# Three tiles of 99 tokens in place of three overlapping tiles of 128 in the variance of a normalisation

## The reference

```python
def _layernorm(x, axis=-1, eps=1e-05):
    m = jnp.mean(x, axis=axis, keepdims=True)
    v = jnp.var(x, axis=axis, keepdims=True)
    return (x - m) / jnp.sqrt(v + eps)
...
h = tokens(x)                            # normalise patches, project, normalise, + embedding
h = concatenate([cls_tok, h], axis=1)    # 16 x 37 tokens of 256 features
h = h + causal_attention(_layernorm(h))  # 16 heads, rotary embedding
h = h + experts(_layernorm(h))           # router, 16 experts that choose 74 tokens each, a shared one
h = h + encoder(_layernorm(h))           # below
h = h + fp4_ffn(_layernorm(h))           # weights and values rounded to fp4 in blocks of 16
...
def encoder(x):
    x = _ln(x, norm_in_g, norm_in_b) + pos_emb
    for l in range(6):
        q, k, v = x @ Wqkv[l].T + bqkv[l]
        o = softmax(mask(q @ k.T / 4)) @ v
        x = _ln(x + o @ Wo[l].T + bo[l], ln1_g[l], ln1_b[l])
        ff = gelu(x @ W1[l].T + b1[l]) @ W2[l].T + b2[l]
        x = _ln(x + ff, ln2_g[l], ln2_b[l])
    return x
```

## Time and profile before

| | |
|---|---|
| three runs | 821.06, 821.38 and 822.22 us |
| median of the runs | 821.38 us |
| span of the profiled execution | 819.1 us |
| PE busy | 801.5 us, 98% of the span |
| PEld busy | 751.4 us, 92% |
| DVE, ACT, POOL busy | 633.9, 460.6 and 251.6 us |
| clock granted to PE | full in all 40 slices of the page |
| DMA | 88.36 MB, 108 GB/s |

### The profile page before, as it was taken

How to read it: one execution, slowest core, us unless ns; L and a number is a source line. 1 busy time by engine, 2 the same in 40 slices (tenths; PEclk the granted TensorE clock), 3 DMA queues, 4 the chain that set the end, 5 groups by cost and what they waited for, 6 DMA issues and landing times.

```text
span 819.1 us, 16629 instructions
## 1 busy us (share of the span) xinstructions
PE 801.5 (98%) x6060; PEld 751.4 (92%) x6060; DVE 633.9 (77%) x1287; ACT 460.6 (56%) x829; POOL 251.6 (31%) x297
## 2 busy tenths in 40 slices
PE   9999999999999999999999999999999999999988
PEld 8998789999999999899999989999998999999758
DVE  5786693778778876778797887878778787876796
ACT  4386424433333336585786777667687767745421
POOL 0002120410111100364366147335525623633020
PEclk9999999999999999999999999999999999999999
DMA  5010946998889812010210021031012103010001
GB/s 191 1 52 1 373 124 253 328 323 310 317 309 337 321 53 107 1 40 14 100 44 0 17 98 38 13 102 38 4 39 72 38 13 102 26 82 1 1 0 30
DMA packets 18290, 88.36 MB, mean 108 GB/s; under 512 B 3120, under 2 KB 7472, under 8 KB 12240
## 3 DMA queue, kind: packets, MB, share of 16 engines
q1 hardware_dynamic: 18256, 87.90, 30.4%
HBM read 85.05 MB, written 2.84 MB: 107 GB/s over the span
## 4 chain that ended last, share of the span: by engine, by line
PE 47%; issue 23%; POOL 18%; DVE 8%; ACT 3%; DMA 1%; POOLq 0%; SPq 0%; DVEq 0%; ACTq 0%
PE bank L1139 14%; POOL W_L L2000 7%; PE bank L1176 6%; POOL HF_L L2058 4%; POOL arena L1981 3%; POOL WQKV_L L2000 3%; PE bank L746 2%; PE bank L872 2%; PE bank L1185 2%; PE bank L722 2%; PE bank L1049 2%; PE bank L788 1%; POOL SQ L2019 1%; PE bank L1123 1%; PE bank L1490 1%
## 5 line engine op out<-in xcount | busy, mean ns | idle before, releaser
L1139 PE MATMUL bank<-arena 128*128 (+1 forms) x1024 | 117.8, 274 | 0.0
L1139 PEld LDWEIGHTS bank<-arena 128*128 128x128 f32 x1024 | 117.4, 192 | 0.0
L1981 POOL TENSOR_TENSOR arena<-arena,srec 111x456 f32<-111x456 f32 x56 | 52.3, 962 | 125.1 <-DVE srec L2153 125.1
L2000 POOL TENSOR_TENSOR W_L<-LW,W_H 128x256 fp32r<-128x256 f32 x96 | 68.5, 752 | 36.9 <-DVE XHL L2589 33.5
L2058 POOL TENSOR_TENSOR HF_L<-arena,HF_H 128x296 fp32r<-128x296 f32 x48 | 43.8, 937 | 76.7 <-ACT HF_H L1896 76.7
L788 PE MATMUL bank<-XHL,W_H 128*128 128x296 f32 x288 | 65.1, 307 | 0.0
L1896 ACT ACTIVATE arena<-bank,vec 128x296 f32<-128x296 f32 x96 | 48.8, 509 | 20.4 <-PE bank L788 15.4
L2012 POOL TENSOR_TENSOR QW<-QW,arena x14 | 22.4, 1600 | 119.0 <-DVE QW L2490 65.6
L1330 PE MATMUL bank<-HF_L,W_H 128*128 128x296 f32 x192 | 57.4, 299 | 0.0
L1330 PE MATMUL bank<-HF_H,W_H 128*128 128x296 f32 x192 | 57.4, 299 | 0.0
L1330 PE MATMUL bank<-HF_H,W_L 128*128 128x296 f32 x192 | 57.3, 299 | 0.0
(11 more groups left out here) (276 smaller groups left out, 2205.4 us busy)
## 6 DMA issues: line engine op xcount, KB each, us to landing
arena<-ew_in SPq DMA_DIRECT2D x16, 2048.0 KB, 9.0
arena<-ew_in SPq DMA_DIRECT2D x16, 1024.0 KB, 7.0
LW<-lw_in SPq DMA_DIRECT2D x12, 1024.0 KB, 5.0
arena<-route SPq DMA_DIRECT2D x32, 185.0 KB, 3.2
LW<-lw_in SPq DMA_DIRECT2D x6, 768.0 KB, 4.3
fp_weights<-arena SPq DMA_DIRECT2D x1, 2048.0 KB, 6.4
arena<-fp_weights SPq DMA_DIRECT2D x1, 2048.0 KB, 7.2
arena<-patches_in SPq DMA_DIRECT2D x2, 864.0 KB, 7.4
```

Of the source, the lines that this page charges most:

```text
L1139: last = mm(o[:, m * CAP:(m + 1) * CAP], w[:, kc, mi * P:(mi + 1) * P], xg(kc, e), start=(kc == 0), stop=(kc == C - 1))
L1981: nc.gpsimd.tensor_tensor(v, v, srec[0:QROWS, s:s + 2, :].unsqueeze(3).to_broadcast([QROWS, 2, C * JH, KEYS]), ALU.mult).then_inc(p_ready, 1)
L2000: last = nc.gpsimd.tensor_tensor(low[:, cols], value[:, cols], high[:, cols], ALU.subtract)
```

## The change

`var_width` is the third part of the tokens of a half, rounded up: 99 for 296 tokens, 96 for 288 patches. The three tiles begin at 0, 99 and 197 (0, 96 and 192 for patches), so that they cover the half with one token taken twice, or none. Every step that reads or writes the tiles gets that width: the weights of the variance and of `patch_stats` have 99 (96) columns in place of 128, their results lie on 99 (96) partitions, the roots, squares, differences and reciprocals work on as many, and the transposes back move the first 99 (96) columns of the identity through weights of 99 (96) rows. The columns that move in the variance stay 64. On every engine the same number of instructions stands in the same order as before, with the same semaphores.

```diff
+        def var_width(nt):
+
+            return -(-nt // 3)
+
         def var_tiles(nt):
 
-            return (0, P), (P, P), (nt - P, nt - 2 * P)
+            w = var_width(nt)
+            return 0, w, nt - w
+
+        def ln_width(seq):
+
+            return var_width(ln_geometry(seq)[1])
...
-                for t, (t0, _) in enumerate(var_tiles(nt)):
+                w = var_width(nt)
+                for t, t0 in enumerate(var_tiles(nt)):
                     for c in range(nch):
                         at = VAR_AT + t * VAR_W
-                        last = mm(ln_bank(seq, h)[:, at:at + VAR_W], sq[:, h, c, t0:t0 + P], ones[:, 0:VAR_W],
+                        last = mm(ln_bank(seq, h)[0:w, at:at + VAR_W], sq[:, h, c, t0:t0 + w], ones[:, 0:VAR_W],
                                   start=(c == 0), stop=(c == nch - 1))
...
-                for t, (t0, _) in enumerate(var_tiles(nt)):
-                    last = nc.tensor.transpose(ln_bank(seq, h)[:, t0:t0 + P], ln_rs[:, h, t:t + 1].to_broadcast([P, P]),
-                                               ident)
+                w = var_width(nt)
+                for t, t0 in enumerate(var_tiles(nt)):
+                    last = nc.tensor.transpose(ln_bank(seq, h)[:, t0:t0 + w], ln_rs[0:w, h, t:t + 1].to_broadcast([w, P]),
+                                               ident[0:w, 0:w])
...
-                    for t, (t0, _) in enumerate(var_tiles(NP_HALF)):
-                        last = mm(bank[5][:, at + t * VAR_W:at + (t + 1) * VAR_W], R[:, h, k, t0:t0 + P], ones_p[:, 0:VAR_W],
+                    w = var_width(NP_HALF)
+                    for t, t0 in enumerate(var_tiles(NP_HALF)):
+                        last = mm(bank[5][0:w, at + t * VAR_W:at + (t + 1) * VAR_W], R[:, h, k, t0:t0 + w], ones_p[:, 0:VAR_W],
                                   start=True, stop=True)
...
-                f(ln_sd[:, h, :], LNB[h][:, VAR_AT:VAR_AT + 3 * VAR_W:VAR_W], ACT.Sqrt, bias=eps1[:, :]).then_inc(ln_std, 1)
+                w = ln_width(seq)
+                f(ln_sd[0:w, h, :], LNB[h][0:w, VAR_AT:VAR_AT + 3 * VAR_W:VAR_W], ACT.Sqrt, bias=eps1[0:w, :]
+                  ).then_inc(ln_std, 1)
...
-                v.reciprocal(ln_rs[:, h, :], ln_sd[:, h, :]).then_inc(ln_rstd, 1)
+                w = ln_width(seq)
+                v.reciprocal(ln_rs[0:w, h, :], ln_sd[0:w, h, :]).then_inc(ln_rstd, 1)
```

More of the change, by code:

```diff
@@ L1567, in enc_root @@
                 act.wait_ge(ln_var, ln_count(LN_ENC, h))
-                f(ln_sd[:, h, :], ln_bank(LN_ENC, h)[:, VAR_AT:VAR_AT + 3 * VAR_W:VAR_W], ACT.Sqrt, bias=eps_sq[:, :], scale=1.0 + EPS
+                w = ln_width(LN_ENC)
+                f(ln_sd[0:w, h, :], ln_bank(LN_ENC, h)[0:w, VAR_AT:VAR_AT + 3 * VAR_W:VAR_W], ACT.Sqrt, bias=eps_sq[0:w, :], scale=1.0 + EPS
                   ).then_inc(ln_std, 1)
@@ L1594, in square_mean @@
                 act.wait_ge(patch_stats_ready, h + 1)
-                f(mean_sq[:, h, :], bank[5][:, MU_AT:MU_AT + 3 * VAR_W:VAR_W], ACT.Square).then_inc(mean_squared, 1)
+                w = ln_width(LN_TOK)
+                f(mean_sq[0:w, h, :], bank[5][0:w, MU_AT:MU_AT + 3 * VAR_W:VAR_W], ACT.Square).then_inc(mean_squared, 1)
             def token_root(h):
@@ L1601, in token_root @@
                 act.wait_ge(ln_var, ln_count(LN_TOK, h))
+                w = ln_width(LN_TOK)
                 for t in range(3):
-                    last = f(ln_sd[:, h, t:t + 1], LNB[h][:, VAR_AT + t * VAR_W:VAR_AT + t * VAR_W + 1], ACT.Sqrt,
-                             bias=eps_var[:, h, t:t + 1])
+                    last = f(ln_sd[0:w, h, t:t + 1], LNB[h][0:w, VAR_AT + t * VAR_W:VAR_AT + t * VAR_W + 1], ACT.Sqrt,
+                             bias=eps_var[0:w, h, t:t + 1])
                 last.then_inc(ln_std, 1)
@@ L2249, in token_eps @@
                 dve.wait_ge(mean_squared, h + 1)
-                link(v.tensor_tensor(eps_var[:, h, :], bank[5][:, EX_AT:EX_AT + 3 * VAR_W:VAR_W], mean_sq[:, h, :], ALU.subtract))
-                v.tensor_scalar(eps_var[:, h, :], eps_var[:, h, :], EPS, EPS * EPS, ALU.mult, ALU.add
+                w = ln_width(LN_TOK)
+                link(v.tensor_tensor(eps_var[0:w, h, :], bank[5][0:w, EX_AT:EX_AT + 3 * VAR_W:VAR_W], mean_sq[0:w, h, :],
+                                     ALU.subtract))
+                v.tensor_scalar(eps_var[0:w, h, :], eps_var[0:w, h, :], EPS, EPS * EPS, ALU.mult, ALU.add
                                 ).then_inc(eps_var_ready, 1)
```

## The result

The changed kernel takes **814.86 us** (median of 5 runs, 814.49 to 815.38) against 821.36 us before (5 runs, 821.06 to 822.22): ratio 0.9921, 95% interval 0.9909 to 0.9933. That is 6.5 us less; forecast were 815.6 us, 5.75 us less, and a range from 812.8 to 819.0.

What follows compares the result with a forecast made beforehand. PE, busy 801.5 of 819.1 us, was taken as the bound wherever no other engine holds it; loop 2.44, front 1.76, router 0.67, entry 0.44 and last layer 0.44 sum to 5.75 us, 821.38 to 815.6 us, range 814.3 to 817.2 (wider 812.8 to 819.0).

Steps and rivals of the forecast that it cites:

- The size of a record: Variance and statistics matmuls: 0.86 ns per weight column, 25 ns a record at width 99, 27.5 at 96; transposes 24 and 26.
- The first rival: 64-column matmuls don't get shorter, as something other than columns sets their pace; only transposes gain, 1.38 us, 820.0 us; chance 0.10.
- LN1 counts, LN2 does not: Encoder loop, eleven phases: a layer's first normalisation saves 1.65 us by variance and 0.79 by transposes, its second nothing.
- The third rival: A layer's second normalisation and other places counted as nothing also pass: 4.0 us more, 811.6 us; chance 0.06.
- LN2 gives nothing: Layer's second normalisation in the loop: variance saving ends at the reciprocal behind DVE's evacuations, transposes' at the next hold; 0 us.
- PE is the one that is waited for: From the first normalisation's variance on, other engines wait for PE, so its savings pass: 2.44 us over eleven phases.
- then scores and hidden layer without a hold: Behind the first normalisation's transposes, PE runs unheld until its 0.34 us wait for the last probabilities.
- front, router and entry: Places ahead of the encoder's loop, where PE's savings were counted at 1.76, 0.67 and 0.44 us.
- I count nothing for it: Final normalisation after the last layer: runs beside ACT and DVE chains that do not wait for it; 0 us.
- The second rival: The loop gives nothing, as a chain through POOL and DMA sets its period; 3.31 us outside it, 818.1 us; chance 0.08.
- The fourth: Rival: each change between 128- and 99-column weights empties the array, 82 changes at 0.16 us, 13.1 us, 828.7 us; chance 0.04.

Runs made afterwards that it cites:

- LN1 alone: Against the kernel before, only the first normalisation of each encoder layer has 99-wide tiles, everything else keeps 128; 818.62 us, ratio 0.9966.
- LN2 alone: Against the kernel before, only the second normalisation of each encoder layer has 99-wide tiles, everything else keeps 128; 820.48 us, ratio 0.9990.

## Why the prediction was right, point by point

**The size of a record** held. Six records of 99 columns save 0.145 us (forecast 0.150), twelve 0.29 (0.30), three transposes 0.072 (0.072). The first rival, that something other than the columns of the load sets the pace, is excluded by 16 moving columns at 0.113 us and by loads of 167 ns. The row that the prediction took the price from could not tell the two sides apart, though: L841 has 111 columns of weights, but it also moves 114, and records of 296 moving columns start 0.249 us apart (L890, L1049), 0.84 ns a column, so that 114 of them would take 0.096 us by themselves (an estimate) where L841 shows 0.096 to 0.097. The price came out right all the same; the 99-column rows, with 64 moving columns, are what shows it. The Trainium skill, "TensorE: Matmul & The Clock Gate", section "LDWEIGHTS (loading the stationary operand)", says that a load's time goes with its columns alone, at 1.2 a nanosecond: by this, as an estimate, 29 columns are worth 24 ns, and the runs show 24 (145 ns over six). Its 107 ns for 128 columns lie under the pace of 112 ns of the traces, and the traces decide. That, and not the section on the issue gap, is the rule that fits these matmuls.

**LN1 counts, LN2 does not** held in its main part, and the loop's total owes something to luck. LN1 alone gives 189 ns of a phase where 222 were counted, LN2 alone 41 where nothing was; up to 736 us that is 2.15 us against 2.44, and 0.59 against 0. The two misses have opposite signs. Together the parts give 244 ns a phase, 14 more than the two alone, and the loop 2.84 us. The third rival (LN2 passes too) asked, by the measured sizes, for 217 ns from LN2. "LN2 gives nothing" was right for its variance and a little too strict for its transposes, of whose 72 ns some 40 come through.

**"PE is the one that is waited for" behind LN1's variance** was right for the variance and wrong in its words for the transposes. The step that fails is "then scores and hidden layer without a hold". There are two holds, in the trace before already. The weight loads of the scores and ACT's key evacuations before (L1878), then the loads after (L845):

```profile
494.27 0.13 PEld L834 LDWEIGHTS bank<-amask 128*111 128x111 bf16 x1
...
500.76 0.13 PEld L834 LDWEIGHTS bank<-amask 128*111 128x111 bf16 x1 [0.23 <-DVE arena L2142]
...
492.58 1.57 ACT L1878 ACTIVATE arena<-bank,kbias,const 128x296 f32<-128x296 f32 x3
```

```profile
491.11 0.13 PEld L845 LDWEIGHTS bank<-amask 128*111 128x111 bf16 x1
...
497.54 0.13 PEld L845 LDWEIGHTS bank<-amask 128*111 128x111 bf16 x1 [0.23 <-DVE arena L2160]
...
489.42 1.57 ACT L1895 ACTIVATE arena<-bank,kbias,const 128x296 f32<-128x296 f32 x3
```

The first scores' load comes 0.12 us behind the end of ACT's last key evacuation (494.27 less 492.58 + 1.57; 491.11 less 489.42 + 1.57), and in all eleven phases of both kernels the same, 113 to 115 ns by the unrounded times. In the other profiles of this document it is 112 to 115 ns too, while the idle time of the loads just ahead goes from 13 ns (16 moving columns) to 83. Those evacuations stand on ACT behind LN1's root, so they move with the variance and not with the transposes. No wait is printed there, because the load would have come less than 0.1 us sooner by itself. What the transposes save goes through DVE: it was idle for them 0.46 us, runs from the scaling on without much pause, and its shift (L2142) is what the fourth scores wait for, 0.23 us in the phase shown and in every second one up to the ninth, 0.16 us at most in the others (in all of them the load starts 52 to 54 ns behind the shift's end). That way 61 ns of the 72 come back. The total was right by another path. That the key evacuations are the cause was read from this constant distance and from the program, in which the scores wait for the keys; no run moved the evacuations by themselves.

**Outside the loop** the terms of front, router and entry held within 0.07 us each. The one that was mis-sized is the final normalisation. "I count nothing for it" was wrong for its second half. Its variance waits 0.41 us for ACT, and what follows on PE stands behind it without a hold; of the 0.36 us that variance and transposes save there, 0.27 stay to the end; what takes the other 0.09 stays open. The timeline of PE after:

```profile
762.82 1.26 PE L756 MATMUL bank<-ones_d,SQ 128*99 128x64 f32 x12 [0.41 <-ACT SQ L1546]
763.92 1.40 PE L1298 MATMUL bank<-arena 128*128 128x352 f32 x4
765.16 0.42 PE L766 MATMUL bank<-const,ln_rs 99*128 99x99 f32 x3
```

The run with all but the layers narrow gains 0.29 us in that stretch. The second rival (the loop gives nothing) fell with LN1 alone at 818.62 us. The fourth (each change of width empties the array) fell with the first row behind a narrow group: L883 at 478.90 us comes 0.55 us behind the start of six records, 0.09 us for each, the last included. The Trainium skill's rule on a drain, "TensorEngine Tiling (Array Packing)", section "Key Properties", speaks of tiling modes; 99 columns in place of 128 do not act like one here.

**The median and the span.** The prediction took its sum off the median. The runs of the changed kernel lie 1.8 us above their own spans, so the span of 819.1 us belongs to a run of some 820.9 us, 0.5 us under the median; the aligned sum of 6.40 us fits the medians' 6.5.

## What to carry to other kernels

Where few columns move, as here, a matmul's record costs its weight columns: overlapping tiles pay for the overlap, and halving the records (one pass in place of two) brought 5.5 us here, trimming their columns 5.1 (the run with wide transposes). Whether a saving counts is decided by who comes last at the next hold: look what the engine that releases the hold was doing just before, since a queue there swallows the saving, and gives it back once that queue is shorter. When a wait is taken away and the time does not fall, the wait was where the slack stood, not where it came from.

## What the runs showed of the hardware that was not expected

- With 64 moving columns the records of a matmul start 0.112 us apart at 128 columns of weights, 0.088 at 99 and 0.085 at 96, and with 16 moving columns 0.112 at 128. From 99 to 128 that is 0.83 ns a column and, as an estimate from the three, some 5 ns that do not go with the columns.
- A transpose of 32-bit numbers loads 128 columns in 136 ns where a matmul takes 191, and its pace goes with what moves: about 0.085 us at 99 columns against 0.109 at 128, with 128 columns of weights both times (the rows of the weights went from 128 to 99 with it, and no run separates the two).
- What the reciprocal costs DVE depends on its place in the row. In the change it starts before the evacuation ahead of it has ended, and the next one starts 0.08 us behind its own start (515.44, 515.52). Between the first and the second of a group nothing overlapped, and the next one started 0.21 us behind it (514.75 to 514.96).
- Executions differ by up to 1.2 us at the first patch product, and little behind it: the aligned starts of two kernels mostly agree to 0.03 us wherever nothing was changed. In three profiles (wide transposes, and both with the variance in one record) 0.34 us were lost behind the router, at the shared expert's first products, and 0.32 to 0.36 us won back at the entry.
